# The scratch of Pool's dynamic DMAs is 8 KB per partition in place of 16 KB

## What is computed

```python
h = relu(layernorm(x))
h = (h @ W_node.T).reshape(N, 4, 32);  e = (edge_attr @ W_edge.T).reshape(E, 4, 32)
att = sum(concat([h[src], h[tgt], e], -1) * a, -1)
att = where(att > 0, att, 0.2 * att)
m = maximum(segment_max(att, tgt), 0.0)
ex = exp(att - m[tgt])
denom = segment_sum(ex, tgt) + (E - deg)[:, None] * exp(-m)
w = ex / denom[tgt]
x = x + segment_sum(w[:, :, None] * h[src], tgt)
```

## Time and profile before

| | us |
|---|---|
| median of 3 runs | 3327.39 (3317.92 to 3330.7) |
| span of the profiled execution, first to last instruction | 2249.8 |
| median less span: not covered by the profile's rows | 1077.6 |
| Pool busy in the span | 1637.4 (73%) |
| VectorE busy | 1601.3 (71%) |
| TensorE busy, matmuls | 1196.2 (53%) |
| ScalarE busy | 620.0 (28%) |

### The profile page before, as it was taken

The page is one execution under the profiler, slowest core; times in us unless marked ns, Lnnn a source line. Parts: engine busy times, 40 slices in busy tenths (PEclk is TensorE's granted clock), DMA queues, the critical chain, the costliest instruction groups (busy, mean ns, idle before and its releaser), DMA issues. The chain is left out here.

```text
span 2249.8 us, 29136 instructions
## 1 busy us (share of the span) xinstructions
PE 1196.2 (53%) x8452; PEld 993.6 (44%) x8453; DVE 1601.3 (71%) x4470; ACT 620.0 (28%) x1207; POOL 1637.4 (73%) x1736
## 2 busy tenths in 40 slices
PE   4565655554555555555556555565545554444442
PEld 4424444444444444444444444444444444444432
DVE  8537777777677777767767677676776776777677
ACT  4422222222222222222222222222222221222223
POOL 6577777777777777777777777777777777777750
PEclk9887777767777767776776776777677776667666
DMA  6463333333333333333333333233332322223234
GB/s 182 142 197 78 94 75 91 84 75 99 75 99 75 75 98 75 94 79 77 92 79 95 75 78 95 75 98 75 75 99 74 97 72 55 56 54 88 54 76 131
DMA packets 87941, 200.00 MB, mean 89 GB/s; under 512 B 30157, under 2 KB 49517, under 8 KB 81383
## 3 DMA queue, kind: packets, MB, share of 16 engines
q0 software_dynamic: 53408, 114.13, 22.8%
q1 hardware_dynamic: 33495, 83.87, 11.2%
q10 hardware_dynamic: 880, 0.13, 0.0%
HBM read 181.70 MB, written 18.15 MB: 89 GB/s over the span
## 5 line engine op out<-in xcount | busy, mean ns | idle before, releaser
L760 POOL DMA_INDIRECT gath<-node_table,src_i x1644 | 1566.1, 953 | 505.6 <-issue 488.2
L840 PE MATMUL bank<-vals,onehot 128*128 128x137 f32 x3288 | 684.1, 385 | 597.7 <-DVE vals L1109 355.6
L840 PEld LDWEIGHTS bank<-vals,onehot 128*128 128x128 f32 x3288 | 632.5, 281 | 624.2 <-DVE vals L1109 365.9
L1143 DVE TENSOR_TENSOR acc<-acc,bank 128x137 f32 x1660 | 494.7, 298 | 416.6 <-PE bank L840 148.2
L915 ACT COPY onehot_t<-ps_oht 128x2048 bf16<-128x2048 bf16 x104 | 194.0, 1865 | 1001.5 <-PE ps_oht L810 977.1
L810 PE MATMUL ps_oht<-ident_b,onehot_b 128*128 128x128 bf16 x1664 | 173.5, 288 | 326.8 <-DVE onehot_b L991 326.8
L924 ACT CAST onehot<-onehot_b 128x384 f32<-128x384 bf16 x622 | 268.1, 475 | 254.8 <-PE bank L840 247.9
L810 PEld LDWEIGHTS ps_oht<-ident_b,onehot_b 128*128 128x128 bf16 x1664 | 157.3, 136 | 335.4 <-DVE onehot_b L991 331.2
L991 DVE TENSOR_TENSOR onehot_b<-bank,rel_s 128x2048 bf16<-128x2048 f32 x104 | 237.2, 2282 | 0.0
L1105 DVE TENSOR_TENSOR vals<-gath,bank 128x2048 f32<-128x2048 f32 (+1 forms) x103 | 234.3, 2275 | 0.2 <-ACT bank L928 0.2
L792 PE MATMUL bank<-eattr,w_eatt 128*32 128x512 f32 x392 | 181.2, 606 | 5.7 <-DMA eattr<-edge_attr_in 3.4
(11 more groups left out here) (191 smaller groups left out, 1007.8 us busy)
## 6 DMA issues: line engine op xcount, KB each, us to landing
eattr<-edge_attr_in SPq DMA_DIRECT2D x49, 1024.0 KB
gath<-node_table,src_i POOLq DMA_INDIRECT x1660
node_table<-onehot_b SPq DMA_DIRECT2D x14, 462.0 KB, 4.2
gath<-x_in SPq DMA_DIRECT2D x14, 448.0 KB, 4.7
edge_scores<-edge_out SPq DMA_DIRECT2D x49, 64.0 KB, 1.9
edge_s<-edge_scores SPq DMA_DIRECT2D x12, 256.0 KB
out_dram<-x_in SPq DMA_DIRECT2D x2, 896.0 KB, 6.9
eattr<-x_in SPq DMA_DIRECT2D x2, 896.0 KB, 4.6
```

Of the source, the lines that this page charges most:

```text
L760: nc.gpsimd.indirect_dma_start(out=gath[:, g.r, a * GS + j, :], out_offset=None, in_=table, in_offset=bass.IndirectOffsetOnAxis(ap=src_i[: ...
L840: last = T.matmul(SUM_BANK[b % 3][:, (j % 3) * ACC:(j % 3 + 1) * ACC], onehot[:, b % 3, j % 3, :], weighted(g, a)[:, j, :], start=True, st ...
L1143: V.tensor_tensor(a_blk, a_blk, SUM_BANK[(j // 3) % 3][:, (j % 3) * ACC:(j % 3 + 1) * ACC], ALU.add).then_inc(s["added"], 1)
```

## The change

One argument is added where the program is made. No instruction, tile, semaphore or DMA is added, removed or moved in its queue. Two things follow from it: the scratch for the descriptors of Pool's DMAs has half the room, and every tile of the kernel in SBUF begins 8,192 bytes lower.

```diff
-    nc = bacc.Bacc("TRN2", target_bir_lowering=False, num_devices=1)
+    nc = bacc.Bacc("TRN2", target_bir_lowering=False, num_devices=1, dynamic_dma_scratch_size=8192)
```

## The result

The changed kernel took 3341.25 us (median of 7 runs, 3335.75 to 3351.4), the kernel before 3325.04 us beside it (7 runs): a ratio of 1.0057, 95% interval 1.0038 to 1.0076. The time lies inside the predicted range of 3312 to 3343 us; the forecast, a difference within 0.5%, does not hold.

What follows compares the result with a forecast made beforehand. Pool's issuing of gathers, 1.25 us apart, was taken to bound the kernel. A span of 2249.8 us plus 0 for half the room and 0 for lower addresses, with 1077.6 us outside it, gave 3327.4 us; range 3312 to 3343 us.

Steps and rivals of the forecast that it cites:

- part one: Descriptor scratch of Pool's DMAs: half the room costs 0 us, since 1,660 gathers and two stores stay as they are.
- the sum's last term: Time outside the profiled span: 3327.4 less 2249.8 us, or 1077.6 us, unexplained by any row and carried over unchanged.
- What bounds the kernel now: Stage 2: Pool's issuing of gathers, one every 1.25 us, 2053 us in all, sets the pace; VectorE follows.
- the signs that the prediction gave for being right: Profile after: gathers near 944 ns, 0.30 us before them; L760 ending about 2180 us; groups 40.3 us apart; span near 2250.
- Rival 1: Pool's gathers: 8 KB holds only two, so each waits for room; +150 us, 3477 us; chance 0.03.
- the scratch must hold 2.68/1.249 = 2.1: Descriptor scratch: 2.68 us from issue to use, at 1.249 us per gather, needs room for two to three gathers.
- Over ten times smaller before it pays: Descriptor scratch: it would have to shrink over ten times before its size costs time; 8 KB estimated at 56 gathers.
- The least room of four gathers for 16 KB: Descriptor scratch: as Pool shows no unexplained longer pause, 16 KB hold at least four gathers at no cost.
- the page's count of descriptors: Descriptor scratch, from the Trainium skill: 16-byte descriptors, nine per DMA engine and transfer, so 16 KB hold 113 gathers.
- Rival 2: Descriptor ring: it comes to its end twice as often, up to +15 us, 3342 us; chance 0.05.
- The addresses: SBUF tiles 8 KB lower: 0 us, as L1012 took 377 to 387 ns on buffers 16.9 KB apart.

Runs made afterwards that it cites:

- e1: The kernel before, nothing edited, run again for a second profile: 3324.90 us against 3327.01 us, ratio 1.000.
- e4: The kernel before with the scratch cut from 16 KB to 1 KB: 2670.18 us against 3327.01 us, ratio 0.8036.
- e7: The kernel before with a scratch of 2 KB: 2465.98 us against 2252.36 us, ratio 1.0947.
- e2: The kernel before with 8 KB scratch and an unused 8 KB tile that keeps all tiles at their old addresses: 3342.43 us against 3327.01 us, ratio 1.0043.
- e9: The changed kernel (8 KB) again, on another chip: 3322.19 us against 3305.32 us for the kernel before, ratio 1.0050.
- e10: The kernel before with a scratch of 12 KB: 3305.51 us against 3305.32 us, ratio 1.0007.
- e13: 8 KB scratch, Pool's wait for the 16th addition moved from the 9th to the 10th gather: 3314.58 us against 3305.19 us for the kernel before, ratio 1.0032.
- e11: The kernel before (16 KB) with Pool pausing after the 7th and 14th gather of each half: 2820.55 us against 3305.32 us, ratio 0.8539.
- e12: The kernel before with a scratch of 1 KB, on another chip: 2650.81 us against 3305.32 us, ratio 0.8023.
- e14: The kernel before with a scratch of 2 KB, on a slower chip: 2992.56 us against 3305.19 us, ratio 0.9062.
- e16: The kernel before with three small chained Pool memsets after each gather: 2981.94 us against 3305.19 us, ratio 0.9028.
- e15: The kernel before with one small Pool memset after each gather: 3357.02 us against 3305.19 us, ratio 1.0175.
- e5: The kernel before (16 KB) with Pool pausing after the 7th and 14th gather of each half: 2596.87 us against 2252.36 us, ratio 1.1530.
- e6: The kernel before (16 KB) with Pool pausing after every 4th gather: 2972.96 us against 2252.36 us, ratio 1.3204.
- e18: The kernel before with two small chained Pool memsets after each gather: 2628.20 us against 2251.96 us, ratio 1.1672.

## Why the prediction was right or wrong

The step that failed, and moved the number, is in part one: "the direct cost of the edit is 1,662 x 0 us, unless a gather then has to wait for room that it had before". No gather waits for room at 8 KB, and still 50 of them start 0.427 us later after their wait, 21 us in the sum; 16.2 us were measured.

**The instrument.** Wrong too, though it cancels in the forecast's number, is the sum's last term: "with the 1077.6 us that lie outside it". Nothing of that size lies outside; the changed kernel's time less its span is 1.9 us, e1's as well. The difference of a third between median and span was the sign that trace and times were not of one behaviour, and I carried it over unchanged in place of doubting the trace. With it fell "What bounds the kernel now": Pool's own pace bounds it on chips of the first kind only. On the others Pool waits for VectorE twice in each group, and ScalarE goes on late in Pool's long run or at its end. So of the signs that the prediction gave for being right only the durations and the fixed step came (gathers of 947 ns with 0.30 us before them, L1012 at 378 to 389 ns), and not the span, the end of L760 at 2180 us or the groups 40.3 us apart.

**Half the room.** That 8 KB are room enough was right: no pause was added, and none is seen down to 4 KB. Rival 1 names a mechanism that exists, with a wrong point and, on the second kind, a wrong sign. It strikes at 2 KB and not at 4 KB, and there and at 1 KB it makes the kernel 9% and 20% faster on the chips of the second kind, slower only on the first (2 KB, 1.095). The working behind the 0 was not sound, however: "the scratch must hold 2.68/1.249 = 2.1" gathers takes it that room comes back as gathers land, yet Pool pauses at 1 KB after every seventh gather and at 2 KB after the fourteenth of a half, many more than the 3.5 that the prediction found under way. "Over ten times smaller before it pays" fails by that too, as 2 KB are an eighth. The least room of four gathers for 16 KB was true and said nothing; the page's count of descriptors came near what e4 and e7 show.

**Coming round.** Rival 2, up to +15 us, gives by chance nearly the measured +16 us, but its mechanism is refuted: 4 KB and 12 KB cost nothing, and the gathers did not get longer (L760 mean 951 ns against 953 in the earlier trace rows).

**The addresses.** The 0 was right as far as the runs can tell: e2 with the old addresses and the change with the new ones both have the long wake and the same 0.4 to 0.6%, and L1012 is as in the earlier trace rows.

**The term that was missing** is Pool's wake after its wait for the additions, 0.427 us longer at exactly this size and this gather, times 50 groups. The prediction had no term for it. In its rows Pool waits for additions only 36 times, 12.7 us in all; on the measured chip it waits there in every group. That the wake goes with the size, and that the lost time lies there, is shown by e9 against e10 on one chip; that nothing else at 8 KB costs time is not, because of e13. I found no row for what Pool does in the 0.427 us; that it is gone at 2, 4, 12 and 16 KB and at the next gather is shown, its cause is open. Whether the 8 KB would cost anything on a chip of the first kind was not run; 12 KB do not.

## What to carry to other kernels

Where the median and the span of the profile differ by more than a few us, the profile shows another behaviour than the one timed, and no sum on it holds; ask for a second profile first. The size of Pool's scratch made no pause here as long as it held the 16 gathers between two changes of semaphore (4 KB and more), and an effect of half a per cent can come from one wake per group on the path. Where Pool issues gathers back to back for long, look for engines that act late on TensorE's finished work, and try pauses or gathers further apart: on three of the five chips seen here that was worth 9 to 20% (e4, e11, e12, e14, e16), though a spacing of 1.283 us cost 2% (e15), and on the other two it cost 9 to 32% (e5, e6, e7, e18).

## What the hardware showed unexpectedly

The same program takes 2252 us on two chips and 3305 to 3327 us on three others, with busy times that agree to within some 8%. On the latter, work that TensorE has finished is not acted on by ScalarE for 13 to 24 us (e1) while Pool issues gathers 1.25 us apart, where it ends at the 8th or 9th gather of a run and not where it ends at the 4th; VectorE acts on finished sums up to 7 us late in e1 and 12 us in e14. With 1.69 us between the gathers ScalarE acts at once (e16). The profiles of these chips also lack more than half of the records of semaphore updates (15,259 in e1 against 35,789 in the trace of before; waits then end by "remote"), except e16's, which has 35,039. Whether updates travel late or something else holds the waiting engines can't be told from the records. Nor can it be told whether the recording itself has a part in it, since the span of every run here was recorded, or whether the chip or a condition of the stretch of runs makes the kind. With a 1 KB scratch both kinds should come close, as Pool then sets the pace for the most part, but it was run on the second kind only: 2651 and 2670 us.
